# A two-layer graph attention kernel: who loads the adjacency matrix, and onto how many partitions at a time

## The chip, the cores and the metric

The kernel runs on one core of a Trainium2 chip. Its time is the device time of one execution in microseconds (us). The kernel before took 2251.49 us as the median of three runs (2243.89 to 2266.31); the execution that was profiled took 2266.05 us, of which the trace's span holds 2264.2 us.

## The reference, cut to what matters

Two attention layers over 8192 nodes with 128 features, the same adjacency matrix in both:

```python
h = jnp.maximum(_layernorm(x, axis=-1), 0.0)
x = x + _L0_gnn_ref(h, adj, ...)
h = jnp.maximum(_layernorm(x, axis=-1), 0.0)
x = x + _L1_gnn_ref(h, adj, ...)

def _L0_gnn_ref(node_features, adjacency_matrix, W, b_W, a_vec, b_a):
    h = node_features @ W.T + b_W
    a1, a2 = (a_vec[:D_OUT], a_vec[D_OUT:])
    e = (h @ a1)[:, None] + (h @ a2)[None, :] + b_a[0]
    e = jnp.where(e > 0, e, 0.2 * e)
    scores = jnp.where(adjacency_matrix > 0, e, jnp.float32(NEG_INF))
    attention = jax.nn.softmax(scores, axis=1)
    return attention @ h
```

`x` is 8192 x 128 float32, `adj` is 8192 x 8192 int32, 256 MB. The second layer differs in names only.

## The kernel before, in words

Since a score is the larger of two sums, each of a row's and a column's term, the exponential of a score is one of two products. So a layer needs no exponential per edge: each edge is a byte of a 0/1 mask in one of two stationary operands (`masks`: sum positive, sum negative), and TensorE multiplies the masks with rows of nodes that were scaled before (`node_rows`). One tile is 128 rows of the adjacency matrix against all 8192 columns: 64 chunks, two matmuls each.

The program has three parts. **Node phase**: for each of 64 tiles of 128 nodes, VectorE, GpSimd (a power, L423), TensorE and ScalarE normalise and project, and the rows go to device memory; each quarter of them comes back rearranged (`load_quadrant`, four loads of 516 KB). **Layer 0**: 64 tiles of adjacency. **Layer 1**: 64 tiles with masks that layer 0 has packed.

A tile of layer 0 works on four row groups r of 32 rows. Partition 32a + i holds row 32r + i of the tile and the columns of quarter a (2048 int32, 8 KB). ScalarE turns each group into bytes (`cast`, L600: `sign_a` from `adj_sb`). `adj_sb` has one buffer for each r and no second one, so a group can be loaded for the next tile once it has been cast for this one. VectorE joins `sign_a` with the sign of the score (`mask_bits`, L824), packs two tiles' masks into `pair_a` (`pack`, L833 on even tiles and L836 on odd ones), transposes blocks (`turn_bits`, L845) and splits the two masks (L853, L860), after which TensorE may start the tile (L538). ScalarE stores `pair_a`, 1 MB, once for two tiles (`store_pair`, L607), and the pack of the next even tile waits until that store has landed. `pair_a` has one buffer.

TensorE's result of a tile is finished on ScalarE (`part_one`, L619) and VectorE (L869 and on), and layer 0 also runs the node work of layer 1 for the finished tiles: VectorE's statistics and `ext` (L790), GpSimd's power (`node_step`, L423), its sum and copy and one scaled half of the rows (`node_rest`, L435, L436, L445), ScalarE's exponential and other half (`node_high`, L586, L588). In `layer_0_tile` ScalarE's order is: `part_one` of the tile before, the store on odd tiles, cast 0 of the tile two ahead, a copy, `z_sign`, cast 1, `z_sign`, cast 2, `node_high` of the tile two behind, cast 3. GpSimd's L445 needs the first result of that `node_high`.

Every engine runs its own list in the order written, with loops over two tiles (four in the node phase); only semaphores hold them. On SP, layer 0 is: for each r, wait for the cast of r and issue the four loads of that group for the next tile; then store and load `x`, and store the node rows. The adjacency of tile 0 is loaded in the node phase, one row group behind the row stores of tiles 16, 32, 35 and 48.

Of the kernel before, what the change touches and what calls it, by code (L numbers as in the profile page):

```python
# [27 lines left out]
TILE = 128  # L28
TILES = NODES // TILE
QUADS = 4  # L30
QROWS = 32
SPAN = NODES // QUADS
RGROUPS = TILE // QROWS
BYTES = 4
BLOCKS = SPAN // (QROWS * BYTES)
# [25 lines left out]
HEAD = 4  # L61
TAIL = 62
NODE_STEP = 4
QUAD_ORDER = (0, 2, 1, 3)


class Tile:
# [21 lines left out]
            eng.wait_ge(sem, self.t - back + 1)  # L89


def sweep(eng, body, trail=0, step=2, head=HEAD):

    end = TILES - step
    for k in range(head):
        body(Tile(k))
    with eng.Fori(head // step, end // step) as u:
        for k in range(step):
            body(Tile(k, u, step))
    for k in range(end, TILES + trail):  # L100
        body(Tile(k))


def gat_kernel(nc, x, adj, w_0, b_w_0, a_vec_0, b_a_0, w_1, b_w_1, a_1, out):
    F32, F16, I8, I32, U32, FP8 = (mybir.dt.float32, mybir.dt.float16, mybir.dt.int8, mybir.dt.int32,
                                   mybir.dt.uint32, mybir.dt.float8e4)
    ALU, ACT, AX = mybir.AluOpType, mybir.ActivationFunctionType, mybir.AxisListType
    ds = bass.ds
# [6 lines left out]
    with ExitStack() as ctx:  # L115
        def sb(name, shape, dt):
            return ctx.enter_context(nc.sbuf_tensor(name, shape, dt))
# [4 lines left out]
        def sem(name):  # L122
            return ctx.enter_context(nc.semaphore(name))


        adj_sb = sb("adj_sb", [128, RGROUPS, SPAN], I32)
        sign_a = sb("sign_a", [128, 2, NODES], I8)
        sign_z = sb("sign_z", [128, 2, NODES], I8)
        pair_a = sb("pair_a", [128, NODES], I8)
# [67 lines left out]
        setup_pe, setup_dve = sem("setup_pe"), sem("setup_dve")  # L197
        x_head, x_rest, rows_free = sem("x_head"), sem("x_rest"), sem("rows_free")
        adj_loaded = [sem(f"adj_loaded_{r}") for r in range(RGROUPS)]
        cast_done = sem("cast_done")  # L200
        packed, pair_stored, pair_loaded = sem("packed"), sem("pair_stored"), sem("pair_loaded")

        class LayerSems:
# [41 lines left out]

        @block.sync
        def _(sp):
            def load_adj(T, r):
                for a in QUAD_ORDER:
                    sp.nop(nofuse=True)  # L250
                    sp.dma_start(adj_sb[QROWS * a:QROWS * (a + 1), r, :],  # L251
                                 adj[ds(T.t * TILE + QROWS * r, QROWS), SPAN * a:SPAN * (a + 1)]) \
                      .then_inc(adj_loaded[r], 16)

            def load_x_old(l, T):
                if T.u is not None or T.k >= 2:
                    sp.wait_ge(S[l].fin, FIN * (T.t - 1))
                sp.nop(nofuse=True)
                sp.dma_start(x_old[:, T.p, :], x_src[l][ds(T.t * TILE, TILE), :]).then_inc(S[l].x_old[T.p], 16)
# [6 lines left out]
            def store_rows(l, T):  # L266
                sp.wait_ge(S[l].low, T.t + 1)
                sp.nop(nofuse=True)
                slot, _ = row_slot(l, T)
                sp.dma_start(rows_dram[l][ds(T.t, 1), :, :].rearrange("o p r -> p (o r)"), row_parts[:, slot, :]) \  # L270
                  .then_inc(S[l].rows_stored[slot], 16)
# [20 lines left out]
            def load_x_group(g):  # L292
                sp.dma_start(x_all[:, first * g:first * (g + 1), :], x_tiles[:, first * g:first * (g + 1), :]).then_inc(x_rest, 16)
# [6 lines left out]
                for g in range(VGROUPS):  # L300
                    load_rows(0, a, g)

            adj_after = [BLOCKS, 2 * BLOCKS, 2 * BLOCKS + 3, 3 * BLOCKS]
            for a in range(QUADS):
                for k in range(BLOCKS * a, BLOCKS * a + NODE_STEP):
                    store_rows(0, Tile(k))
                    if k in (0, 2):
                        load_x_group(2 + k // 2)
                    if k in adj_after:
                        load_adj(Tile(0), adj_after.index(k))  # L310
                if a:
                    load_quadrant(a - 1)
                with sp.Fori(BLOCKS // NODE_STEP * a + 1, BLOCKS // NODE_STEP * (a + 1)) as u:
                    for k in range(NODE_STEP):
                        store_rows(0, Tile(k, u, NODE_STEP))
# [10 lines left out]
                sp.dma_start(pair_a[:], mask_dram[ds(T.n, 1), :, :].rearrange("o p c -> p (o c)")).then_inc(pair_loaded, 16)  # L326

            def layer_0_tile(T):
                if T.plus(1).exists:
                    for r in range(RGROUPS):  # L330
                        sp.wait_ge(cast_done, RGROUPS * T.t + r + 1)
                        load_adj(T.plus(1), r)
                if T.plus(-3).exists:
                    store_x_new(0, T.plus(-3))
                    load_x_old(0, T.plus(-1))
                if T.plus(-4).exists:
                    store_rows(1, T.plus(-4))
# [58 lines left out]
        def _(pool):  # L396
# [5 lines left out]
                               pattern=[[-1, 128]], channel_multiplier=1).then_inc(ident_ready, 1)  # L402
# [3 lines left out]
            def build_picks():  # L406
                for r in range(RGROUPS):
                    pool.tensor_copy(pick_s[:, r, :].rearrange("p (a i) -> p a i", a=QUADS),
                                     ident[:, QROWS * r:QROWS * (r + 1)].unsqueeze(1).to_broadcast([128, QUADS, QROWS])) \
                        .then_inc(picks_ready, 1)  # L410
                for b in range(BLOCKS):
                    pool.tensor_copy(pick_t[:, b, :].rearrange("p (a i) -> p a i", a=QUADS),
                                     t_columns[:, b, :].unsqueeze(2).to_broadcast([128, QUADS, QROWS])).then_inc(picks_ready, 1)

            build_picks()
            nat_v = nat[:].rearrange("p (c t) -> p c t", c=2)

            def node_step(l, T):
# [28 lines left out]

            for l in range(LAYERS):
                if l:
                    pool.wait_ge(S[0].nat_ps, 1)  # L450
                    pool.wait_ge(S[0].coefs, 2)
                    pool.wait_ge(limits, n_limits)

                def body(T):
                    if l and T.u is None and T.k == TILES - 2:
                        pool.wait_ge(S[0].turned, TILES)
                        build_picks()
                    if T.exists:
                        node_step(l, T)
                    rest = T.plus(l - 1)  # L460
                    if rest.exists:
                        node_rest(l, rest)

                sweep(pool, body, trail=1 - l, step=[NODE_STEP, 2][l])


        @block.tensor
# [103 lines left out]
        def _(act):  # L571
# [22 lines left out]
            def cast(T, r):  # L594

                if r == 0 and (T.u is not None or T.k >= 2):
                    act.wait_ge(S[0].edge_bits, T.t - 1)
                    act.wait_ge(packed, T.t - 1)
                act.wait_ge(adj_loaded[r], 16 * QUADS * (T.t + 1))
                nc.scalar.activation(sign_a[:, T.p, SPAN * r:SPAN * (r + 1)], adj_sb[:, r, :], ACT.Sign, scale=-1.0) \  # L600
                  .then_inc(cast_done, 1)

# [647 lines left out]
```

## Time and profile before

| | us |
|---|---|
| median of three runs | 2251.49 |
| the profiled execution | 2266.05 |
| its span | 2264.2 |
| TensorE matmuls busy | 2015.0 (89%) |
| VectorE busy | 1664.7 (74%) |
| ScalarE busy | 1134.8 (50%) |
| GpSimd busy | 347.0 (15%) |
| node phase, about | 0 to 157 |
| layer 0, about | 157 to 1300 |
| layer 1, about | 1360 to 2264 |

A busy share is an average over three parts with different limits, so each part is read by itself: the DMA row of the page is full in layer 0 and nearly empty in layer 1. In the rows of groups, the number before a "mean ns of one" is the busy sum, and what stands behind the bar is the idle time of the engine just before such an instruction with what ended it. A wait that hangs on several semaphores is put down to the one that came last by the profile.

### The profile page before, as it was taken

How to read it: one execution, taken by the hardware profiler on the slowest of the kernel's cores; microseconds unless marked ns; L12 is line 12 of the kernel's file. 1: busy time of each engine (PE TensorE's matmuls, PEld its weight loads, DVE VectorE, ACT ScalarE, POOL GpSimd, SP SyncE). 2: the span in 40 equal slices, each digit the busy share in tenths (PEclk: the TensorE clock that was granted, in tenths of full speed). 3: DMA queues.
4: the chain of work that ended last, by engine and by line, in shares of the span. 5: the costliest groups of instructions: out<-in, count | busy, mean ns of one | idle time of the engine just before them, and what ended most of it. 6: DMA issues, size and time to landing. Idle time of an engine off the chain costs nothing.

```text
span 2264.2 us, 49373 instructions
## 1 busy us (share of the span) xinstructions
PE 2015.0 (89%) x16866; PEld 1710.1 (76%) x16866; DVE 1664.7 (74%) x2685; ACT 1134.8 (50%) x1097; POOL 347.0 (15%) x496
## 2 busy tenths in 40 slices
PE   5455889889998898988988979999999999999998
PEld 3234677777777777777877868888888888888887
DVE  6564778778878777787787767777777777777774
ACT  4455667777767676676777433322222223333331
POOL 6440122212222222222222210000000000000000
PEclk9997899999999999999999989999999999999999
DMA  5659999999999999999999681111111111111110
GB/s 145 161 141 243 254 292 280 288 294 309 309 304 269 282 277 278 286 273 288 282 285 296 180 189 47 46 46 46 46 46 46 46 46 46 46 46 46 45 45 11
DMA packets 121683, 390.99 MB, mean 173 GB/s; under 512 B 25137, under 2 KB 74545, under 8 KB 80689
## 3 DMA queue, kind: packets, MB, share of 16 engines
q1 hardware_dynamic: 117040, 357.01, 58.2%
q10 hardware_dynamic: 4608, 33.56, 3.7%
q8 instruction: 18, 0.29, 0.1%
q14 instruction: 17, 0.13, 0.0%
HBM read 331.62 MB, written 58.85 MB: 172 GB/s over the span
## 4 chain that ended last, share of the span: by engine, by line
PE 59%; DMA 25%; DVE 5%; issue 4%; ACT 3%; SPq 2%; DVEq 0%; ACTq 0%; POOL 0%; POOLq 0%
PE acc L538 58%; DMA adj_sb<-in_adj_dram 12%; DMA mask_bytes<-pair_a 11%; DVE masks L845 2%; DMA node_rows<-row_parts 2%; ACT sign_a L600 2%; SPq L251 1%; DVE ext L790 1%; ACT part_a L619 1%; PE ps_h L490 0%; ACT b_and_d L586 0%; ACT row_parts L588 0%; DMA masks<-in_x_dram 0%; DVE row_parts L797 0%; SPq L277 0%
## 5 line engine op out<-in xcount | busy, mean ns | idle before, releaser
L538 PE MATMUL acc<-node_rows,masks 128*128 128x258 f16 x16384 | 1907.9, 278 | 133.7 <-ACT part_a L619 76.0
L538 PEld LDWEIGHTS acc<-node_rows,masks 128*128 128x128 fp8e4 x16384 | 1624.3, 99 | 396.6 <-issue 142.1
L600 ACT ACTIVATE sign_a<-adj_sb 128x2048 int8<-128x2048 int32 x256 | 487.4, 1904 | 142.3 <-DMA adj_sb<-in_adj_dram 137.7
L613 ACT ACTIVATE sign_z<-t_row,neg_s 128x2048 int8<-128x2048 f32 x256 | 503.9, 1994 | 1.0 <-DVE masks L845 1.0
L619 ACT ACTIVATE part_a<-acc,coef_a 128x258 f32<-128x258 f32 x128 | 60.1, 470 | 721.4 <-PE acc L538 721.4
L809 DVE TENSOR_SCALAR sign_z<-t_row,neg_s 128x2048 int8<-128x2048 f32 x256 | 327.0, 1279 | 7.4 <-issue 6.8
L845 DVE STREAM_TRANSPOSE masks<-sign_z 128x2048 uint32<-128x2048 uint32 x128 | 295.0, 2305 | 0.1
L869 DVE SCALAR_TENSOR_TENSOR part_ac<-acc,coef_c,part_a 128x258 f32<-128x258 f32 x128 | 62.1, 485 | 297.8 <-ACT part_a L619 297.6
L435 POOL TENSOR_TENSOR h_sum<-h_sum,ext 128x128 f32<-128x128 f32 x126 | 113.1, 898 | 795.5 <-DVE ext L790 791.8
L833 DVE TENSOR_SCALAR pair_a<-sign_a 128x2048 uint32<-128x2048 uint32 x32 | 39.3, 1227 | 179.8 <-DMA mask_bytes<-pair_a 179.8
L824 DVE SCALAR_TENSOR_TENSOR sign_z<-sign_z,sign_a 128x2048 uint32<-128x2048 uint32 x64 | 146.3, 2285 | 19.7 <-ACT sign_z L613 19.7
L853 DVE TENSOR_SCALAR masks<-masks 128x2048 uint32<-128x2048 uint32 x128 | 155.9, 1218 | 0.1
L860 DVE TENSOR_SCALAR masks<-masks 128x2048 uint32<-128x2048 uint32 x128 | 155.8, 1217 | 0.1
L824 DVE SCALAR_TENSOR_TENSOR sign_z<-sign_z,pair_a 128x2048 uint32<-128x2048 uint32 x64 | 146.3, 2286 | 1.4 <-ACT sign_z L613 1.3
L423 POOL TENSOR_TENSOR rstd<-var_eps,minus_half 128x1 f32<-128x1 f32 x128 | 125.3, 980 | 139.8 <-DVE var_eps L726 139.5
L490 PE MATMUL ps_h<-w_ext,centred_t 128*128 128x133 f32 x256 | 78.0, 397 | 73.1 <-ACT centred_t L575 69.5
L490 PEld LDWEIGHTS ps_h<-w_ext,centred_t 128*128 128x128 f32 x256 | 51.9, 253 | 94.0 <-ACT centred_t L575 71.8
L797 DVE SCALAR_TENSOR_TENSOR row_parts<-ext,b_and_d,row_parts 128x129 f16<-128x129 f32 x256 | 89.0, 349 | 44.6 <-ACT row_parts L588 44.2
L586 ACT ACTIVATE b_and_d<-ext 128x2 f32<-128x2 f32 x128 | 25.6, 200 | 179.3 <-DVE ext L790 132.0
L445 POOL TENSOR_SCALAR row_parts<-ext,b_and_d 128x129 f16<-128x129 f32 x64 | 75.3, 1176 | 17.3 <-ACT b_and_d L586 17.2
L836 DVE SCALAR_TENSOR_TENSOR pair_a<-sign_a,pair_a 128x2048 uint32<-128x2048 uint32 x32 | 73.0, 2282 | 0.0
L485 PE MATMUL ps_t<-ident,centred 128*128 128x128 f32 x128 | 49.4, 388 | 19.6 <-DVE centred L723 18.4
(81 smaller groups left out, 580.2 us busy)
## 6 DMA issues: line engine op xcount, KB each, us to landing
adj_sb<-in_adj_dram SPq DMA_DIRECT2D x1024, 256.0 KB, 10.4
mask_bytes<-pair_a ACTq DMA_DIRECT2D x32, 1024.0 KB, 10.8
pair_a<-mask_bytes SPq DMA_DIRECT2D x32, 1024.0 KB, 4.8
node_rows<-row_parts SPq DMA_DIRECT2D x128, 129.0 KB, 8.1
node_rows<-node_rows SPq DMA_DIRECT2D x32, 516.0 KB, 12.3
x_old<-in_x_dram SPq DMA_DIRECT2D x64, 64.0 KB, 11.9
x_after_layer<-x_new SPq DMA_DIRECT2D x64, 64.0 KB, 12.3
x_old<-x_after_layer SPq DMA_DIRECT2D x64, 64.0 KB, 1.8
```

What stands on the lines that cost most here:

```text
L423: pool.tensor_tensor(rstd[:, T.p, :], var_eps[:, T.p, :], minus_half[:], ALU.pow).then_inc(S[l].rstd, 1)
L435: pool.tensor_tensor(h_sum[:], h_sum[:], ext[:, T.p, 0:DIM], ALU.add).then_inc(S[l].h_sum, 1)
L490: pe.matmul(ps_h[:, 0:EXT], centred_t[:, T.p, :], w_ext[l][:], start=True, stop=True).then_inc(S[l].h_raw, 1)
L538: mm = pe.matmul(acc[T.p][s][:, 0:ROW], stationary[s][:, c // BYTES, c % BYTES, :], node_rows[:, c, ROW * s:ROW * (s + 1)], start=(c == 0) ...
L600: nc.scalar.activation(sign_a[:, T.p, SPAN * r:SPAN * (r + 1)], adj_sb[:, r, :], ACT.Sign, scale=-1.0) \
L613: nc.scalar.activation(sign_z[:, T.p, SPAN * r:SPAN * (r + 1)], t_row[:], ACT.Sign, scale=-1.0, bias=neg_s[:, ds(RGROUPS * T.t + r, 1)]).t ...
L797: ins = nc.vector.scalar_tensor_tensor(out=row_parts[:, slot, ROW * s + PART:ROW * (s + 1)], in0=ext[:, T.p, 0:PART], scalar=b_and_d[:, T. ...
L809: nc.vector.tensor_scalar(sign_z[:, T.p, SPAN * r:SPAN * (r + 1)], t_row[:], neg_s[:, ds(RGROUPS * T.t + r, 1)], -1.0, ALU.is_gt, ALU.mult) \
L824: nc.vector.scalar_tensor_tensor(out=bits, in0=bits, scalar=LOW_Z_WORD[T.p], in1=edges, op0=ALU.bitwise_xor, op1=ALU.bitwise_and).then_inc ...
L845: nc.vector.transpose(g2[:, T.p, :].bitcast(U32).rearrange("p (b r i) -> p r b i", r=RGROUPS, i=QROWS), sign_z[:, T.p, :].bitcast(U32).rea ...
L853: nc.vector.tensor_scalar(g1[:, T.p, :].bitcast(U32), words, SHIFT_G1[T.p], EDGE_WORD, ALU.logical_shift_left, ALU.bitwise_and).then_inc(S ...
L860: nc.vector.tensor_scalar(words, words, SHIFT_G2[T.p], EDGE_WORD, ALU.logical_shift_left, ALU.bitwise_and).then_inc(S[l].g_ready, 1)
```

## The change

The adjacency loads move from SP's queue to GpSimd's. One indirect DMA loads a whole row group, 1 MB onto 128 partitions: the matrix is seen as 32768 rows of 2048 elements, and partition p takes the row whose number stands in `adj_index` for it. The numbers are made once (an `iota` and three small corrections) in two copies, and after a tile's loads the other copy is moved on by two tiles. The bytes, their places and the single buffer per row group are as before; 1024 loads become 256.

```diff
-            def load_adj(T, r):
-                for a in QUAD_ORDER:
-                    sp.nop(nofuse=True)
-                    sp.dma_start(adj_sb[QROWS * a:QROWS * (a + 1), r, :],
-                                 adj[ds(T.t * TILE + QROWS * r, QROWS), SPAN * a:SPAN * (a + 1)]) \
-                      .then_inc(adj_loaded[r], 16)
...
-                    if k in adj_after:
-                        load_adj(Tile(0), adj_after.index(k))
...
             def layer_0_tile(T):
-                if T.plus(1).exists:
-                    for r in range(RGROUPS):
-                        sp.wait_ge(cast_done, RGROUPS * T.t + r + 1)
-                        load_adj(T.plus(1), r)
                 if T.plus(-3).exists:
...
+            def load_adj(T):
+
+                pool.wait_ge(index_ready, QUADS + T.t)
+                for r in range(RGROUPS):
+                    if T.u is not None or T.k:
+                        pool.wait_ge(cast_done, RGROUPS * (T.t - 1) + r + 1)
+                    pool.nop(nofuse=True)
+                    pool.indirect_dma_start(out=adj_sb[:, r, :], out_offset=None, in_=adj_rows_of_2048,
+                                            in_offset=bass.IndirectOffsetOnAxis(ap=adj_index[:, T.p, r:r + 1], axis=0)) \
+                        .then_inc(adj_loaded[r], 16)
+                if T.u is None and T.k == 0:
+                    pool.engine_nop().then_inc(index_ready, 1)
+                else:
+                    pool.tensor_scalar(adj_index[:, 1 - T.p, :], adj_index[:, 1 - T.p, :], float(2 * QUADS * TILE), 1.0,
+                                       ALU.add, ALU.mult).then_inc(index_ready, 1)
...
             for l in range(LAYERS):
                 if l:
+                    load_adj(Tile(1))
                     pool.wait_ge(S[0].nat_ps, 1)
                     pool.wait_ge(S[0].coefs, 2)
                     pool.wait_ge(limits, n_limits)
+                    for k in range(2, LOADS_AHEAD):
+                        load_adj(Tile(k))
 
                 def body(T):
...
+                    if l == 0 and T.u is None and T.k == HEAD - 1:
+                        load_adj(Tile(0))
+                    if l and T.plus(LOADS_AHEAD).exists:
+                        load_adj(T.plus(LOADS_AHEAD))
                     if T.exists:
                         node_step(l, T)
```

`LOADS_AHEAD` is 4. The lines of the file move by 19 behind the GpSimd part (ScalarE's cast is L600 before and L619 after).

GpSimd's loop of layer 0 before, one of its two tiles (a row is a line of the kernel, the operation, result and operands, and the semaphores it waits for; the names ending in 1 are layer 1's node work):

```order
L423 TENSOR_TENSOR rstd<-var_eps,minus_half 128x1 [waits var_eps_1,ext_1]
L435 TENSOR_TENSOR h_sum<-h_sum,ext 128x128 [waits ext_1,h_sum_1]
L436 ISA
L436 COPY nat<-ext 128x2
L445 TENSOR_SCALAR row_parts<-ext,b_and_d 128x129 [waits b_and_d_1,rows_stored_1_1]
```

The same loop now, from the end of the even tile (L457 is L445 of before) to where the odd tile's power (L435, before L423) follows:

```order
L457 TENSOR_SCALAR row_parts<-ext,b_and_d 128x129 [waits rows_stored_1_0]
L414 REGISTER_ALU
L417 ISA [waits index_ready]
L419 DMA adj_sb<-in_adj_dram,adj_index 128x2048 [waits cast_done]
L417 REGISTER_ALU
L419 DMA adj_sb<-in_adj_dram,adj_index 128x2048 [waits cast_done]
L417 REGISTER_ALU
L419 DMA adj_sb<-in_adj_dram,adj_index 128x2048 [waits cast_done]
L417 REGISTER_ALU
L419 DMA adj_sb<-in_adj_dram,adj_index 128x2048 [waits cast_done]
L425 TENSOR_SCALAR adj_index<-adj_index 128x4
L432 REGISTER_ALU
```

The four loads stand between one tile's L457, ahead of which GpSimd waits for ScalarE's `b_and_d`, and the next tile's L435.

SP's loop of layer 0 before, the last row group of one tile and what follows it:

```order
L251 ISA [waits cast_done]
L251 DMA adj_sb<-in_adj_dram 32x2048
L251 ISA
L251 DMA adj_sb<-in_adj_dram 32x2048
L251 ISA
L251 DMA adj_sb<-in_adj_dram 32x2048
L251 ISA
L251 DMA adj_sb<-in_adj_dram 32x2048
L262 ISA
L264 ISA [waits fin_0]
L264 DMA x_after_layer<-x_new 128x128
L259 ISA [waits fin_0]
```

And one tile of it now:

```order
L258 ISA [waits fin_0]
L258 DMA x_after_layer<-x_new 128x128
L253 ISA [waits fin_0]
L253 DMA x_old<-in_x_dram 128x128
L264 ISA [waits low_1]
L264 DMA node_rows<-row_parts 128x516
```

SP waits for no cast any more.

## Rows read from the trace of the kernel before

**Rows 1.** The page: busy time, slices of the span, DMA.
```profile
PE 2015.0 (89%) x16866; PEld 1710.1 (76%) x16866; DVE 1664.7 (74%) x2685; ACT 1134.8 (50%) x1097; POOL 347.0 (15%) x496
...
DMA  5659999999999999999999681111111111111110
```

**Rows 2.** Stretches: us, busy by engine (instructions), clock, DMA share, GB/s.
```profile
197.00:490.00 293.00, 244.69 (x2049) 205.86 (x2050) 223.72 (x327) 204.28 (x160) 53.80 (x57) 0.94 1.02 277
490.00:1290.00 800.00, 718.30 (x6032) 610.38 (x6030) 629.80 (x970) 561.13 (x459) 193.14 (x185) 0.94 1.00 282
...
1364.00:2264.00 900.00, 890.73 (x7962) 777.36 (x7960) 651.92 (x806) 256.91 (x183) 0.00 (x0) 1.00 0.13 44
```

**Rows 3.** Chain of waits in two stretches: start us, us, what.
```profile
377.22 12.93 DMA adj_sb<-in_adj_dram
390.17 1.92 ACT sign_a L600
...
663.82 10.86 DMA mask_bytes<-pair_a
...
698.25 11.29 DMA mask_bytes<-pair_a
```

**Rows 4.** Cast 3 of tiles 1, 3 and 63, from the timeline.
```profile
191.34 1.91 ACT L600 ACTIVATE sign_a<-adj_sb 128x2048 int8<-128x2048 int32 x1 [2.67 <-DMA adj_sb<-in_adj_dram]
...
230.13 1.91 ACT L600 ACTIVATE sign_a<-adj_sb 128x2048 int8<-128x2048 int32 x1 [2.54 <-DMA adj_sb<-in_adj_dram]
...
1275.92 1.89 ACT L600 ACTIVATE sign_a<-adj_sb 128x2048 int8<-128x2048 int32 x1
```

**Rows 5.** Timeline around one even tile: start us, us, engine, line.
```profile
698.77 1.91 ACT L600 ACTIVATE sign_a<-adj_sb 128x2048 int8<-128x2048 int32 x1 [0.24 <-issue]
...
706.33 1.90 ACT L600 ACTIVATE sign_a<-adj_sb 128x2048 int8<-128x2048 int32 x1
...
709.57 1.23 DVE L833 TENSOR_SCALAR pair_a<-sign_a 128x2048 uint32<-128x2048 uint32 x1 [6.75 <-DMA mask_bytes<-pair_a]
...
715.12 1.21 DVE L860 TENSOR_SCALAR masks<-masks 128x2048 uint32<-128x2048 uint32 x1
...
716.58 4.03 PE L538 MATMUL acc<-node_rows,masks 128*128 128x258 f16 x18 [4.00 <-ACT part_a L619]
```

**Rows 6.** The same timeline, the tile after it, ScalarE and GpSimd.
```profile
717.60 1.33 POOL L423 TENSOR_TENSOR rstd<-var_eps,minus_half 128x1 f32<-128x1 f32 x1 [1.03 <-DVE var_eps L726]
...
728.11 1.34 POOL L435 TENSOR_TENSOR h_sum<-h_sum,ext 128x128 f32<-128x128 f32 x1 [9.18 <-DVE ext L790]
728.49 0.19 ACT L586 ACTIVATE b_and_d<-ext 128x2 f32<-128x2 f32 x1
729.63 1.35 POOL L445 TENSOR_SCALAR row_parts<-ext,b_and_d 128x129 f16<-128x129 f32 x1
```

**Rows 7.** The page: DMA issues, KB each, median us from issue to landing.
```profile
adj_sb<-in_adj_dram SPq DMA_DIRECT2D x1024, 256.0 KB, 10.4
mask_bytes<-pair_a ACTq DMA_DIRECT2D x32, 1024.0 KB, 10.8
pair_a<-mask_bytes SPq DMA_DIRECT2D x32, 1024.0 KB, 4.8
...
x_old<-x_after_layer SPq DMA_DIRECT2D x64, 64.0 KB, 1.8
```

**Rows 8.** GpSimd in the node phase, and what VectorE waits for there.
```profile
18.04 0.55 POOL L435 TENSOR_TENSOR h_sum<-h_sum,ext 128x128 f32<-128x128 f32 x1 [0.51 <-DVE ext L790]
...
30.86 0.29 DVE L710 BATCH_NORM_STATS2 stats<-masks 128x6 f32<-128x128 f32 x1 [5.92 <-DMA masks<-in_x_dram]
```

**Rows 9.** Chain of waits in the node phase.
```profile
91.75 15.59 DMA node_rows<-row_parts
```

**Rows 10.** Timeline where layer 0 opens, GpSimd and SP.
```profile
154.97 0.25 POOL L436 COPY nat<-ext 128x2 f32<-128x2 f32 x1
...
162.72 37.55 SPq L251 DMA_DIRECT2D adj_sb<-in_adj_dram  x35
```

More of the change, by code:

```diff
@@ L63 @@
 NODE_STEP = 4
-QUAD_ORDER = (0, 2, 1, 3)
+LOADS_AHEAD = 4
 class Tile:
@@ L89, in wait_before, with sweep @@
             eng.wait_ge(sem, self.t - back + 1)
-def sweep(eng, body, trail=0, step=2, head=HEAD):
-    end = TILES - step
+def sweep(eng, body, trail=0, step=2, head=HEAD, tail=None):
+    end = TILES - (tail or step)
     for k in range(head):
@@ L126, in gat_kernel @@
         adj_sb = sb("adj_sb", [128, RGROUPS, SPAN], I32)
+        adj_index = sb("adj_index", [128, 2, RGROUPS], I32)
         sign_a = sb("sign_a", [128, 2, NODES], I8)
@@ L199, in gat_kernel @@
         adj_loaded = [sem(f"adj_loaded_{r}") for r in range(RGROUPS)]
-        cast_done = sem("cast_done")
+        cast_done, index_ready = sem("cast_done"), sem("index_ready")
         packed, pair_stored, pair_loaded = sem("packed"), sem("pair_stored"), sem("pair_loaded")
@@ L301, in load_quadrant @@
                     load_rows(0, a, g)
-            adj_after = [BLOCKS, 2 * BLOCKS, 2 * BLOCKS + 3, 3 * BLOCKS]
             for a in range(QUADS):
@@ L415, in _ @@
             build_picks()
+            pool.iota(adj_index[:].rearrange("p b r -> p (b r)"), pattern=[[QUADS * TILE, 2], [QUADS * QROWS, RGROUPS]], base=0,
+                      channel_multiplier=QUADS).then_inc(index_ready, 1)
+            pool.wait_ge(index_ready, 1)
+            for a in range(1, QUADS):
+                part = adj_index[QROWS * a:QROWS * (a + 1), :, :].rearrange("p b r -> p (b r)")
+                pool.tensor_scalar(part, part, float(a - QUADS * QROWS * a), 1.0, ALU.add, ALU.mult).then_inc(index_ready, 1)
+                pool.wait_ge(index_ready, a + 1)
+            adj_rows_of_2048 = adj.rearrange("n (a c) -> (n a) c", a=QUADS)
+            def load_adj(T):
[12 more added lines that the diff above has]
+                                       ALU.add, ALU.mult).then_inc(index_ready, 1)
             nat_v = nat[:].rearrange("p (c t) -> p c t", c=2)
@@ L462, in body @@
                         node_rest(l, rest)
-                sweep(pool, body, trail=1 - l, step=[NODE_STEP, 2][l])
+                sweep(pool, body, trail=1 - l, step=[NODE_STEP, 2][l], tail=[NODE_STEP, LOADS_AHEAD][l])
         @block.tensor
@@ L598, in cast @@
                     act.wait_ge(packed, T.t - 1)
-                act.wait_ge(adj_loaded[r], 16 * QUADS * (T.t + 1))
+                act.wait_ge(adj_loaded[r], 16 * (T.t + 1))
                 nc.scalar.activation(sign_a[:, T.p, SPAN * r:SPAN * (r + 1)], adj_sb[:, r, :], ACT.Sign, scale=-1.0) \
```

## The prediction

> **What bounds the kernel now.** Start with the page [rows 1]: a TensorE busy for 89% says little here, while the DMA row reads 9 (90% or more) from the fourth slice to the twenty-second, which is layer 0, and 1 behind it. Then the stretches [rows 2]. Layer 1 is TensorE's: 64 tiles in 900 us, 14.06 us each, at full clock and a DMA share of 0.13. It has no adjacency load and the change cannot touch it. Layer 0 has a DMA share of 1.00 to 1.02 at 277 to 282 GB/s, and a clock of 0.94.
>
> The chain of waits [rows 3] splits layer 0 in two. Up to about 490 us it runs in a ring: cast 3 of a tile (1.92), SP's issue, a load that takes about 13 us to land (12.93 in the row), cast 3 of the next tile. From there to 1290 us a 1 MB mask store of 10.9 to 11.3 us comes once in two tiles, 34.4 us apart (663.82 to 698.25): VectorE's pack of the even tile stands 6.75 us until the store has landed, its last mask ends at 716.33, and TensorE starts at 716.58 after 4.00 us of idleness [rows 5]. That row names ScalarE's `part_a`, but the code wants only the `part_a` of two tiles before, so I take the mask, which ended 0.25 us earlier, as what let TensorE go. From cast 3 of tile 3 to cast 3 of tile 63 it is (1275.92 - 230.13) / 60 = 17.43 us a tile [rows 4]. Both halves are transfers that share the DMA engines: the loads crowd the store and the store crowds the loads.
>
> A tile moves 4 MB of adjacency, half a mask store (0.5 MB), `x` in and out (64 KB each) and 129 KB of rows: 4.75 MB in 17.2 us (half of 34.4), or 3.6 us per MB. For comparison, layer 1's `pair_a` load has the shape of the new loads, 1 MB as 8 KB on each of 128 partitions, and with nothing beside it lands in 4.8 us; 64 KB land in 1.8 [rows 7]. So 960 KB more cost 3.0 us, 3.2 us per MB.
>
> **Part 1: when the load is issued.** This is where I expect the change to be decided. Before, SP issues the load of group 0 as soon as cast 0 has freed the buffer, and there remains almost a tile's time for it. Now it is issued by GpSimd, in program order behind L445 (L457 in the new file), which scales a node's rows and waits for ScalarE's `b_and_d`. ScalarE computes `b_and_d` only behind cast 2. Loads of groups 0, 1 and 2 whose buffers have long been free stand behind it. That closes a ring, once per tile:
>
> - GpSimd issues group 0's load, and it lands: 4.8 us if it is alone, by the `pair_a` load [rows 7], plus what software issue costs over SP's, which no row shows. From below nothing; from above, two GpSimd instructions of layer 0, 2.7. I take one, 1.3, since the issue walks 128 partitions as L435 (1.34) and L445 (1.35) do [rows 6].
> - ScalarE from the start of cast 0 to the end of cast 2, with a copy and two `z_sign` between: 698.77 to 708.23, 9.46 us [rows 5]. Nothing can be taken out, since it runs without a gap.
> - `b_and_d` 0.19 and L445 1.35 [rows 6], about 1.6 with the semaphores.
>
> Sum: 4.8 + 1.3 + 9.5 + 1.6 = 17.2 us. ScalarE does cast 3 and `part_one` while the load is under way, and both are hidden. On odd tiles ScalarE issues the mask store behind cast 3 and `part_one`, about 3 us after cast 2 ends, and GpSimd has issued group 0 after 1.6 + 1.3 us: the two start together. If the store's MB goes entirely beside group 0, it adds 3.2 us; if behind it, nothing. The store lands in 10.8 us beside loads against the 4.8 of a lone MB [rows 7], so sharing is real; I take 2.4, three quarters. The mean is 17.2 + 1.2 = **18.4 us a tile**, 0.97 more than now, and for the 60 tiles from 3 to 63 that is +58 us. Between the ends: 11.1 + 4.8 = 15.9 us (neither issue nor store costs anything) and 11.1 + 4.8 + 2.7 + 1.6 = 20.2 us (two instructions' worth of issue, the store's whole 3.2 on every other tile).
>
> The other limits stay under this. TensorE is busy 718.3 of 800 us, 15.7 us a tile at 17.43, part of it at the lower clock. The DMA engines' load is 4.75 MB by 3.2 to 3.6, 15.2 to 17.1 us. VectorE is busy 629.8 of 800 us, 13.7 us a tile [rows 2].
>
> **Part 2: what 128 partitions bring.** Before, four loads of 256 KB land in 10.4 us each in a queue, so no row tells the rate that the matrix could have. The bracket is 3.6 us per MB as now and 3.2 as the `pair_a` load has it. It shortens the ring of the first stretch, which this change replaces by the ring of part 1 anyway. Over the stretches bound by these loads and stores the trace moves 277 and 282 GB/s [rows 2].
>
> The Trainium skill ("SBUF — State Buffer", "Door 1: The DMA port swizzle") says that a transfer onto 32 partitions reaches 8 of 16 ports, with 189 GB/s measured at 1 MB, and that only a single transfer over all 128 reaches every port. This trace does not agree for quarters in a row: with them it moves half as much again. By that rule the matrix would have been at half rate and the change would win, which is the first rival; by the rows a spread MB gains 0.4 us at most.
>
> **Part 3: GpSimd and VectorE.** L435 takes 0.55 us in the node phase [rows 8] and 1.34 in layer 0 [rows 6], beside VectorE's long instructions. So GpSimd is slowed there, and its four issues would be too; that is why the price above is 1.3 and not 0.6. Its own list is four issues at 1.3, the index at 1.3, L423 1.33, L435 1.34, L436 0.25 and L445 1.35 [rows 6, 10], 10.8 us a tile, under 17. The power L423, now behind the issues, is due when VectorE reaches `ext`; between the end of L423 and the next `ext` the rows leave 728.11 - 718.93 = 9.2 us [rows 6], more than the 6.5 of issues and index.
>
> The Trainium skill ("SBUF — State Buffer", the warning that VectorE blocks DMAs) says that a VectorE instruction in a two-port mode keeps GpSimd from writing its DMAs' descriptors, and that DMAs from SP or ScalarE are immune. L435's two durations agree that GpSimd is held up there; for a DMA no row here shows it. It speaks against this change, and what it would do is the second rival.
>
> **Part 4: the beginning.** Node phase: three times the chain runs through a row store that lands late, the longest 15.59 us [rows 9], because 1 MB of adjacency (2 in that one) and 2 MB of rows stand ahead in SP's queue. Without the adjacency that is 4 x 3.6 = 14 us less. Against that, all 4 MB now come at about 21 us, just before VectorE waits for `x` until 30.86 [rows 8]: between nothing and the same 14 us, and the four issues hold up GpSimd's power by 5 us, inside that wait. I take the 14, together 0. Opening of layer 0: SP's loads of tile 1 begin at 162.72, GpSimd could issue from 155.2 [rows 10], beside 2 MB of rows: 6 MB at 3.6 land by 177, cast 3 of tile 1 was at 191.34 [rows 4], -13. Tiles 2 and 3 come without the ring (GpSimd issues them with no node work between): 4.5 MB by 3.6, 16.3 against (230.13 - 191.34) / 2 = 19.4, -6. Sum of the part: about **-20**, with ends -34 (`x` is not delayed) and +5 (the opening gains nothing and the issues are not covered).
>
> SP loses 1024 issues, which are credited with nothing, since the transfer behind each hides them. Its `x` loads and stores now share the engines with another queue instead of standing in line. The removed pack wait (6.75 us) does not come back as time, since the ring is longer than what it held up.
>
> **Sum.** -20 + 58 = +38 us: 2266.05 becomes 2304 for such an execution, and from the median, which is 14.6 lower, **2290 us**, 1.7% slower.
>
> **Rivals.**
> 1. *Faster.* The ring is shorter than now: software issue costs about as much as SP's, and the store falls behind group 0's load. Then a tile is 15.9 to 17.2 us, middle 16.6, and 60 tiles save 50, with the beginning 70 us: 2181. For it: the store bound more than half of layer 0, and that is gone; the first stretch was bound by loads, and if their shape held them back, spread loads leave the engines free for the store. Against it: 9.5 us of ScalarE work and 4.8 us of landing stand in one ring and leave only 1.5 us to lose. It decides from issue plus store under 1.5 us a tile. By the port rule of the Trainium skill (its page on SBUF) it would come out this way. Chance 0.28.
> 2. *Much slower.* Each issue on GpSimd takes 2.5 us or more under VectorE, or the indirect loads move at less than 1 MB in 3.6. A tile is then 20 to 21 us: -20 + 60 x 3 = +160, 2410. For it: the stretching of L435. Against it: right behind L445 VectorE waits for ScalarE's `part_a`, so the first issue at least finds it idle. By the Trainium skill's warning on blocked descriptors (same page) it would come out this way. Chance 0.17.
> 3. *Nothing.* The ring comes out at 17.4 to 17.9 us, and the beginning pays for it: 2231 to 2260. This also covers that loads spread over 128 partitions are as fast as the four quarters in a row, so that one full DMA queue is exchanged for another. Chance 0.10.
>
> **How the numbers follow.** About 1% (22 us) is what this measurement can tell from no change. The forecast has 0.45, of which 0.08 lies within 1%. Faster 0.28, same 0.10 + 0.08 = 0.18, slower 0.37 + 0.17 = 0.54. The forecast's own range is 2255 to 2325 (ring 17.8 to 19.0). To leave out no more than 2 in 10, the range reaches down to 2190, which takes in most of the first rival, and up to 2410, the second.
>
> **What would show it.** Right: ScalarE's cast 0 waits for `adj_sb` on nearly every tile, 3 us or more, and casts 1 and 2 hardly; GpSimd's first load of a tile starts right behind L457; cast 3 to cast 3 is 17.5 to 19 us; VectorE's L833 no longer waits for the store; the DMA row in layer 0 falls below 9. Wrong: the wait at cast 0 stays under 2 us (rival 1); GpSimd's issues last over 2 us or all four casts wait (rival 2); cast 3 of tile 1 is not near 178 us, or `x` is late by more than 14 us (part 4).

## The result, and the profile after

The changed kernel took 2299.14 us as the median of four runs (2297.34 to 2300.41), beside 2255.56 us for the kernel before in four runs: a ratio of 1.022, with a 95% interval of 1.017 to 1.026. The forecast was 2290 us, slower by 1.7%.

The page of the changed kernel, its busy row, slices and the three queues that moved data:

```profile
PE 2033.5 (88%) x16866; PEld 1719.1 (75%) x16866; DVE 1674.4 (73%) x2685; ACT 1124.7 (49%) x1097; POOL 763.3 (33%) x819
...
DMA  5558777777677777767777581111111111111110
...
q0 software_dynamic: 36864, 268.45, 29.7%
q1 hardware_dynamic: 67888, 88.51, 13.1%
q10 hardware_dynamic: 4608, 33.56, 4.6%
```

Against [rows 1], the DMA row of layer 0 has fallen from 9 to 7 while the kernel became slower: the transfers got cheaper, and the DMA engines stand idle part of the time. GpSimd's busy time has doubled. The stretches say the same (answers to [rows 2], same columns):

```profile
197.00:490.00 293.00, 256.15 (x2118) 215.80 (x2117) 224.66 (x338) 195.66 (x159) 168.02 (x141) 0.94 0.72 271
490.00:1290.00 800.00, 693.21 (x5694) 582.94 (x5693) 603.09 (x912) 532.38 (x436) 464.88 (x393) 0.93 0.71 272
```

The DMA share went from 1.00 to 0.71 in the long stretch for nearly the same rate (282 and 272 GB/s), and TensorE's matmuls there from 6032 to 5694: fewer tiles in the same 800 us. Where the time goes is in the waits (engine and line, who it waited for, us in total, times, longest):

```profile
ACT sign_a L619 <- DMA adj_sb<-in_adj_dram,adj_index: 320.3, 67, 8.4
...
POOL row_parts L457 <- ACT b_and_d L605: 199.5, 59, 5.1
...
DVE pair_a L852 <- DMA mask_bytes<-pair_a: 36.0, 30, 5.1
```

ScalarE's casts now wait 4.8 us each, 67 times, which is about once in a tile (before it was 137.7 us in 98 waits). GpSimd waits for ScalarE's `b_and_d`, 59 times. VectorE's pack (L833 before, L852 now) waits 36.0 us where it waited 179.8. A ring of two engines and a transfer has taken the place of the store: GpSimd issues the load, ScalarE casts it and then computes `b_and_d`, and GpSimd waits for that before the next load. One pair of tiles in the timeline (start us, us, engine, line; in brackets the idle time before and its end):

```profile
702.51 0.38 POOL L457 TENSOR_SCALAR row_parts<-ext,b_and_d 128x129 f16<-128x129 f32 x1 [2.86 <-ACT b_and_d L605]
...
703.39 1.60 POOL L419 DMA_INDIRECT adj_sb<-in_adj_dram,adj_index  x1 [0.50 <-issue]
...
704.44 0.34 ACTq L626 DMA_DIRECT2D mask_bytes<-pair_a  x1
...
711.89 1.91 ACT L619 ACTIVATE sign_a<-adj_sb 128x2048 int8<-128x2048 int32 x1 [7.03 <-DMA adj_sb<-in_adj_dram,adj_index]
...
719.45 1.90 ACT L619 ACTIVATE sign_a<-adj_sb 128x2048 int8<-128x2048 int32 x1
721.25 0.19 ACT L605 ACTIVATE b_and_d<-ext 128x2 f32<-128x2 f32 x1
...
721.64 0.38 POOL L457 TENSOR_SCALAR row_parts<-ext,b_and_d 128x129 f16<-128x129 f32 x1 [5.09 <-ACT b_and_d L605]
...
722.76 1.68 POOL L419 DMA_INDIRECT adj_sb<-in_adj_dram,adj_index  x1 [0.74 <-issue]
...
729.28 1.91 ACT L619 ACTIVATE sign_a<-adj_sb 128x2048 int8<-128x2048 int32 x1 [3.74 <-DMA adj_sb<-in_adj_dram,adj_index]
...
739.97 1.59 POOL L419 DMA_INDIRECT adj_sb<-in_adj_dram,adj_index  x1 [0.50 <-issue]
```

From the first load's issue to the next tile's: 722.76 to 739.97 is 17.21 us without a store (an even tile's group 0), 703.39 to 722.76 is 19.37 us with the store issued a microsecond behind (an odd one's). Over tiles 6 to 62 of the trace the two kinds take 17.18 and 19.59 us in the mean. Over the layer (answers to [rows 4]: cast 3 of tile 3 and of tile 63):

```profile
208.42 1.91 ACT L619 ACTIVATE sign_a<-adj_sb 128x2048 int8<-128x2048 int32 x1 [0.53 <-DMA adj_sb<-in_adj_dram,adj_index]
...
1310.56 1.90 ACT L619 ACTIVATE sign_a<-adj_sb 128x2048 int8<-128x2048 int32 x1
```

Tile 3 is reached 230.13 - 208.42 = 21.7 us sooner than before. From there 60 tiles take 18.37 us each instead of 17.43, +56.3 us, and what follows is equal (2264.2 - 1275.9 = 988.3 us before, 2298.6 - 1310.6 = 988.0 now). -21.7 + 56.3 = +34.6, against a difference of the two spans of 34.4 us.

### The profile page after: what moved, and what is told of

Its sections match the earlier page's. It is cut to its first block, busy times and chain, and to the rows that moved or that the text cites. A ratio compares the mean times of both kernels' runs of the same rounds, so it can differ in the third digit from the quotient of the medians.

```text
span 2298.6 us, 46859 instructions
## 1 busy us (share of the span) xinstructions
PE 2033.5 (88%) x16866; PEld 1719.1 (75%) x16866; DVE 1674.4 (73%) x2685; ACT 1124.7 (49%) x1097; POOL 763.3 (33%) x819
## 4 chain that ended last, share of the span: by engine, by line
PE 48%; DMA 21%; issue 14%; ACT 11%; DVE 3%; SPq 1%; POOL 1%; DVEq 0%; POOLq 0%; ACTq 0%
PE acc L557 47%; DMA adj_sb<-in_adj_dram,adj_index 16%; ACT sign_a L619 6%; ACT sign_z L632 3%; DMA node_rows<-row_parts 3%; PE ps_h L509 1%; DMA masks<-in_x_dram 1%; DVE ext L809 1%; ACT centred_t L594 1%; SPq L271 0%; DMA mask_bytes<-pair_a 0%; ACT b_and_d L605 0%; DVE masks L864 0%; ACT row_parts L607 0%; ACT part_a L638 0%
## 5 line engine op out<-in xcount | busy, mean ns | idle before, releaser
L619 ACT ACTIVATE sign_a<-adj_sb 128x2048 int8<-128x2048 int32 x256 | 486.3, 1901 | 320.4 <-DMA adj_sb<-in_adj_dram,adj_index 320.3
L419 POOL DMA_INDIRECT adj_sb<-in_adj_dram,adj_index x256 | 424.9, 1660 | 124.1 <-issue 94.6
L828 DVE TENSOR_SCALAR sign_z<-t_row,neg_s 128x2048 int8<-128x2048 f32 x256 | 327.5, 1281 | 5.9 <-issue 5.3
L864 DVE STREAM_TRANSPOSE masks<-sign_z 128x2048 uint32<-128x2048 uint32 x128 | 294.9, 2304 | 0.1
L509 PE MATMUL ps_h<-w_ext,centred_t 128*128 128x133 f32 x256 | 88.2, 441 | 193.8 <-ACT centred_t L594 186.3
L843 DVE SCALAR_TENSOR_TENSOR sign_z<-sign_z,sign_a 128x2048 uint32<-128x2048 uint32 x64 | 146.3, 2285 | 4.2 <-ACT sign_z L632 4.2
L843 DVE SCALAR_TENSOR_TENSOR sign_z<-sign_z,pair_a 128x2048 uint32<-128x2048 uint32 x64 | 146.3, 2286 | 1.4 <-ACT sign_z L632 1.3
L435 POOL TENSOR_TENSOR rstd<-var_eps,minus_half 128x1 f32<-128x1 f32 x128 | 105.6, 827 | 9.9 <-DVE var_eps L745 4.5
L457 POOL TENSOR_SCALAR row_parts<-ext,b_and_d 128x129 f16<-128x129 f32 x64 | 26.5, 414 | 199.5 <-ACT b_and_d L605 199.5
L809 DVE SCALAR_TENSOR_TENSOR ext<-ps_h,rstd,bias 128x133 f32<-128x133 f32 x128 | 43.4, 339 | 44.7 <-PE ps_h L509 44.5
```

The lines of the kernel that those rows point to most:

```text
L419: pool.indirect_dma_start(out=adj_sb[:, r, :], out_offset=None, in_=adj_rows_of_2048, in_offset=bass.IndirectOffsetOnAxis(ap=adj_index[:, ...
L435: pool.tensor_tensor(rstd[:, T.p, :], var_eps[:, T.p, :], minus_half[:], ALU.pow).then_inc(S[l].rstd, 1)
L509: pe.matmul(ps_h[:, 0:EXT], centred_t[:, T.p, :], w_ext[l][:], start=True, stop=True).then_inc(S[l].h_raw, 1)
L828: nc.vector.tensor_scalar(sign_z[:, T.p, SPAN * r:SPAN * (r + 1)], t_row[:], neg_s[:, ds(RGROUPS * T.t + r, 1)], -1.0, ALU.is_gt, ALU.mult) \
L843: nc.vector.scalar_tensor_tensor(out=bits, in0=bits, scalar=LOW_Z_WORD[T.p], in1=edges, op0=ALU.bitwise_xor, op1=ALU.bitwise_and).then_inc ...
L864: nc.vector.transpose(g2[:, T.p, :].bitcast(U32).rearrange("p (b r i) -> p r b i", r=RGROUPS, i=QROWS), sign_z[:, T.p, :].bitcast(U32).rea ...
```

## The experiments

Twelve kernels were built, each run four times (six for the two with three early groups, ten for the changed kernel with the small store). "Tile" is (cast 3 of tile 63 - cast 3 of tile 3) / 60 in each one's trace; a ratio is to the kernel before on the same chip.

| kernel | us | ratio, 95% interval | tile, us |
|---|---|---|---|
| changed kernel | 2299.1 | 1.022, 1.017 to 1.026 | 18.37 |
| three groups early | 2104.2 | 0.934, 0.931 to 0.938 | 15.09 |
| group 0 early | 2114.3 | 0.939, 0.935 to 0.944 | 15.33 |
| three early, tile 0 later | 2103.9 | 0.932, 0.929 to 0.936 | 15.10 |
| 0.95 us ahead of the loads | 2314.1 | 1.026, 1.020 to 1.031 | 18.57 |
| 0.95 us behind the loads | 2300.5 | 1.019, 1.013 to 1.024 | 18.38 |
| 2.8 us ahead of the loads | 2427.1 | 1.081, 1.077 to 1.086 | 20.46 |
| changed, small store | 2237.0 | 0.994, 0.992 to 0.997 | 17.42 |
| before, small store | 2203.1 | 0.976, 0.969 to 0.983 | 15.87 |
| SP, 1 MB on 128 partitions | 2134.1 | 0.947, 0.943 to 0.952 | 15.66 |
| the same, strided source | 2134.1 | 0.950, 0.947 to 0.954 | 15.60 |
| SP, quarters, contiguous | 2275.5 | 1.013, 1.006 to 1.020 | 17.52 |
| SP, 256 KB on 128 partitions | 2111.6 | 0.941, 0.937 to 0.945 | 15.24 |

**Is it the place of the loads in GpSimd's list?** Two kernels move loads ahead of the waits, each for the tile five ahead instead of four; behind L457 that is the same tile as before. The first, shortened (the call in the loop's body goes):

```diff
-LOADS_AHEAD = 4
+LOADS_AHEAD = 5
 def node_rest(l, T):
+    load_adj(T.plus(LOADS_AHEAD), [0, 1])
     pool.wait_ge(S[l].ext, T.t + 1)
 ...
+    load_adj(T.plus(LOADS_AHEAD), [2])
     pool.wait_ge(S[l].b_and_d, T.t + 1)
 ...
     pool.tensor_scalar(row_parts[...], ...).then_inc(S[l].high_d, 1)
+    load_adj(T.plus(LOADS_AHEAD), [3])
```

> The changed kernel with GpSimd's loads taken out of one block: groups 0 and 1 of the next tile are issued ahead of the wait for ext, group 2 ahead of the wait for ScalarE's b_and_d, group 3 behind the scaled rows (L457). Ring theory (a tile is GpSimd's issue behind L457, landing, ScalarE's casts 0 to 2, b_and_d, L457: 18.37 us): the ring is gone, a tile falls to what engines and transfers allow, 15.5 to 16.5 us, and the run takes 2299 - 60 x 2.2 = 2165 us (2150 to 2190). Rival 1, software-issued loads move too slowly or take too long to issue: no more than 1% changes, 2280 to 2300. Rival 2, eight more microseconds of GpSimd work beside VectorE slow the tile, wherever they stand: no change.

It took 2104 us, 8.5% less than the changed kernel and 6.6% less than the kernel before. Direction and place are as the ring says; the size is well past the 2150 to 2190 us expected. The stretch and the timeline of this kernel:

```profile
490.00:1100.00 610.00, 595.33 (x5296) 516.85 (x5294) 556.40 (x849) 497.61 (x404) 427.87 (x362) 1.00 0.88 330
```

```profile
699.13 1.56 POOL L416 DMA_INDIRECT adj_sb<-in_adj_dram,adj_index  x1
...
701.98 1.03 POOL L416 DMA_INDIRECT adj_sb<-in_adj_dram,adj_index  x1 [1.29 <-ACT sign_a L630]
703.00 1.90 ACT L630 ACTIVATE sign_a<-adj_sb 128x2048 int8<-128x2048 int32 x1
...
709.10 1.80 POOL L416 DMA_INDIRECT adj_sb<-in_adj_dram,adj_index  x1 [0.15 <-issue]
```

Loads now leave GpSimd soon after casts have freed the buffers (the second row waited for a cast), and no cast of the steady tiles waits a microsecond or more. TensorE is busy 98% of the stretch at full clock, and a tile of 15.09 us is near the 14.06 us of layer 1 plus the node matmuls. The kernel has become TensorE's in both layers, and moves 330 GB/s at a DMA share of 0.88.

The second moves group 0 alone (`[0]` ahead of `ext`, `[1, 2, 3]` behind L457):

> Only group 0's load is issued early (ahead of the wait for ext); groups 1 to 3 stay behind L457 as in the changed kernel. Ring theory: the ring now runs through group 1, 6.5 us of issue and landing + 5.6 us from cast 1 to the end of cast 2 + 1.3 = 13.4 us, shorter than TensorE's tile, so most of the gain of the run with three early groups is there already: 2160 to 2200 us. If the ring holds for every group (the order of the loads does not matter, their number behind L457 does), about a quarter of that gain: 2265. Rivals of slow transfers or of GpSimd's load: 2280 to 2300.

2114 us, below the expected range too: 185 of the 195 us come with one load of four. It is group 0's load behind L457 that closed the ring, as the arithmetic of 13.4 us for group 1 said. What waits now is cast 1, more than 1 us in 56 of 60 tiles, and cast 0 in 7. The three loads still there cost about 10 us, and GpSimd's added work is all still present.

**A dose on the ring and beside it.** A memset in a buffer of its own, in one kernel ahead of the four loads, in its twin behind them:

```diff
 if l and T.plus(LOADS_AHEAD).exists:
+    pool.memset(spare[:], 0.0)       # one kernel
     load_adj(T.plus(LOADS_AHEAD))
+    pool.memset(spare[:], 0.0)       # the other
```

> The changed kernel with one more GpSimd instruction, a memset of 128 x 1024 float32 in a buffer of its own, between L457 and the first load of each steady tile. Ring theory: its duration d (1 us or a little more; the trace will tell) lengthens every tile: 2299 + 60 d, about 2365 us. Rival, transfers bound the tile and GpSimd has slack: 2299. Rival, GpSimd's work beside VectorE costs wherever it stands: the same loss as in the twin with the memset elsewhere.

> The twin: the same memset behind the four loads and the index update, ahead of the power L435. Ring theory: off the ring, 2299 us within 0.5%. Rival, GpSimd's work beside VectorE costs wherever it stands: as slow as the kernel with the memset ahead of the loads.

Beside the ring it costs nothing (2300.5). On the ring it cost 15 us where 57 were expected (0.95 us by its trace, 60 times). The trace of the kernel with the dose shows where the rest went:

```profile
727.41 0.38 POOL L458 TENSOR_SCALAR row_parts<-ext,b_and_d 128x129 f16<-128x129 f32 x1 [4.78 <-ACT b_and_d L607]
...
727.74 0.94 POOL L477 MEMSET spare<- 128x1024 f32 x1
...
728.86 1.38 POOL L420 DMA_INDIRECT adj_sb<-in_adj_dram,adj_index  x1 [0.18 <-issue]
```

From the end of the scaled rows to the load there are 1.07 us with the memset and were 0.50 to 0.74 without, so half of it filled an issue gap. From the load's issue to cast 0 the tiles then take 0.2 to 0.3 us less in the mean. On even tiles the first issue is shorter (1.41 us for 1.67 in the mean, here 1.38 for 1.68), on odd ones it is longer (1.91 for 1.60) and the load lands sooner all the same, so this second part is seen and not explained. In all 0.75 of 0.95 us were absorbed. A longer dose, a copy of 128 x 3072 to int8 at the same place, should then cost its length less a constant:

> The memset between L457 and the first load gave 0.2 us a tile for 0.95 us of work, since the first load's issue got shorter beside it and an issue gap of 0.5 to 0.7 us was filled. Here a longer GpSimd instruction (a copy of 128 x 3072 int8, about 3 us) stands there. Ring theory with 0.7 us absorbed once: 2299 + 60 x (d - 0.7), 2430 us for d = 3. If GpSimd had slack at that place and the small dose showed it: under 2330.

2427.1 us. Its trace has these casts 3 of tile 3 and tile 63:

```profile
210.00 1.91 ACT L621 ACTIVATE sign_a<-adj_sb 128x2048 int8<-128x2048 int32 x1 [0.50 <-DMA adj_sb<-in_adj_dram,adj_index]
...
1437.82 1.90 ACT L621 ACTIVATE sign_a<-adj_sb 128x2048 int8<-128x2048 int32 x1
```

The copy takes 2.74 us in the median and 2.79 in the mean, and the tile grew by 20.46 - 18.37 = 2.09 us, its mean length less 0.7. With d = 2.74 to 2.79 the expected formula gives 2421 to 2424. From the small dose to the long one, 1.84 us more of work made the tile 1.90 longer: the slope is the ring's, and both doses lost the same 0.7 to 0.75 us. The growth is not even, though: even tiles grew by 3.1 us (17.18 to 20.30) and odd ones by 1.1 (19.59 to 20.70). The later loads meet the store at another moment, which may be why; it was not tried.

**What does the store cost?** The store and its load in layer 1 cut from 8 KB to 64 bytes a partition:

```diff
-act.dma_start(mask_dram[ds(T.n, 1), :, :]..., pair_a[:])
+act.dma_start(mask_dram[ds(T.n, 1), :, 0:64]..., pair_a[:, 0:64])
```

> The changed kernel with the mask store (and the load of it in layer 1) cut from 1 MB to 8 KB in all, 64 bytes a partition; it leaves out most of the packed mask. Ring theory: odd tiles lose the 2.2 us by which the store lengthens group 0's landing (8.5 against 6.5 us), every tile takes the even tile's 17.2 us: 2299 - 60 x 1.1 = 2233 us. If the store runs in time that is idle anyway: 2299.

2237.0 us for 2233 expected, and a tile of 17.42 us, close to the even tile's 17.21. The mean over odd tiles fell from 19.59 to 17.77 us, over even ones it stayed at 17.18. The other side, the same cut in the kernel before:

> The kernel before with the mask store and its load cut to 64 bytes a partition; it leaves out most of the packed mask. If the store bounded the second part of layer 0, the wait of 6.75 us in two tiles goes and the loads have the engines to themselves: tiles of 15.6 us instead of 17.4, 2251 - 60 x 1.8 = 2145 us. If the loads bound everything anyway: a tenth fewer bytes, 2225.

This one is not settled in size. Its four runs spread from 2167 to 2239 us, and the profiled one is the fastest of them, with a tile of 15.87 us. All four lie below the lowest of the eleven runs of the kernel before beside them (2244), so the cut does something, but the median lies between the two expectations. In its trace the queue is still full (share 1.03) and ScalarE waits 161 us for loads, so the loads were the next bound. Nor did the pack's wait go as expected: VectorE still waits 99 us in 31 times (179.8 before), since the 8 KB store lands in 8.8 us in the median beside those loads, against 10.8 for 1 MB. What held the pack up was mostly the full queue, and not the store's own bytes.

**What was fast: the partitions, the source or the size?** The kernel with three early groups came out 61 us under its expectation (2104 for 2165). Its 330 GB/s are 3.2 us per MB, the low end of the prediction's 3.2 to 3.6, and that at a DMA share of 0.88, so the transfers must be cheaper still. Four kernels keep SP as the issuer, with its order and waits, and vary the load alone. The first:

```diff
-for a in QUAD_ORDER:
-    sp.dma_start(adj_sb[QROWS * a:QROWS * (a + 1), r, :],
-                 adj[ds(T.t * TILE + QROWS * r, QROWS), SPAN * a:SPAN * (a + 1)])
+sp.dma_start(adj_sb[:, r, :],
+             adj.rearrange("n (a c) -> (n a) c", a=QUADS)[ds(T.t * (QUADS * TILE) + 128 * r, 128), :])
```

> The kernel before with SP issuing each row group as one direct load of the same contiguous MB onto 128 partitions (partition p takes the p-th 8 KB), so issuer, order and times of issue are as before and only the shape is that of the change. It leaves out the arrangement of the rows, so the masks belong to other edges. If the shape frees the transfers (3.2 instead of 3.6 us per MB or better): the ring of loads in the first stretch and the wait for the store shrink, 2170 to 2210 us. If quarters in a row were as fast as a spread MB: 2240 to 2265, no change against before.

2134 us, below the 2170 to 2210 expected: the shape alone is worth 5% when issuer, order and waits stay. The next takes `adj[ds(T.t * TILE, TILE), SPAN * r:SPAN * (r + 1)]` as the source:

> As the run with one direct 1 MB load from SP per row group, but the MB is 128 rows of 8 KB that stand 32 KB apart in device memory, the run before had them in one piece. It leaves out the arrangement of the rows. If the spread over 128 partitions made that run fast: the same, 2134 us (2120 to 2150). If it was the contiguous source: back towards the kernel before, 2220 to 2260.

And four quarters again, each from one contiguous piece (`[... + 128 * r + QROWS * a, QROWS]`):

> The other half of that question: SP loads four quarters of 256 KB onto 32 partitions each, as the kernel before, but each quarter is one contiguous piece of the same contiguous MB. It leaves out the arrangement of the rows. If partitions decide: as the kernel before, 2235 to 2265 us. If the source decides: 2134.

The strided source changes nothing (2134.1) and the quarters bring the old time back, even 1.3% more (2275.5, and 10 us above the range; why was not tried). It is the spread over 128 partitions and not the source. The last keeps the partitions and cuts the size, four loads of 512 columns:

> SP loads each row group in four DMAs of 256 KB, each over all 128 partitions with 2 KB a partition. It leaves out the arrangement of the rows. If the number of partitions decides and not the size of a DMA: near 2134 us, 2130 to 2170 for four times the issues and smaller pieces. If the size of a DMA (1 MB against 256 KB) decides: as the kernel before, 2235 to 2265.

2111.6 us, faster than with 1 MB and below the expected range: the size of a DMA is not what made 1 MB fast. The same stretch, 490 to 1100 us, of the kernels before, with 1 MB, with contiguous quarters and with spread 256 KB:

```profile
490.00:1100.00 610.00, 547.99 (x4617) 466.13 (x4615) 476.17 (x736) 433.24 (x352) 146.33 (x140) 0.94 1.02 288
```

```profile
490.00:1100.00 610.00, 578.97 (x5083) 500.94 (x5081) 529.61 (x817) 478.11 (x388) 163.85 (x156) 0.99 0.87 317
```

```profile
490.00:1100.00 610.00, 537.50 (x4619) 456.26 (x4618) 479.48 (x736) 437.75 (x352) 130.32 (x140) 0.98 1.03 289
```

```profile
490.00:1100.00 610.00, 593.78 (x5283) 516.10 (x5281) 548.80 (x848) 496.33 (x404) 170.27 (x161) 1.00 0.98 329
```

Quarters fill the DMA engines (1.02, 1.03) at 288 and 289 GB/s, wherever they read from. Spread 1 MB loads move 317 GB/s at 0.87 and are then not the bound: TensorE is busy 95% of the stretch. The strided kernel's stretch has 318 GB/s at 0.89.

The Trainium skill ("SBUF — State Buffer", "Door 1: The DMA port swizzle") gives the rule that only a transfer over all 128 partitions reaches all ports. These runs agree in direction, and disagree with half the rate for 32 partitions: with quarters the core moved 288 GB/s. The Trainium skill ("DMA: Bandwidth & Descriptors", "Rules for kernel authors") also asks for 1 MiB or more a DMA beside 128 partitions, for maximum bandwidth. Here the kernel with 256 KB was faster than the one with 1 MB, 2111.6 against 2134.1, but its DMA engines worked more for each byte (329 GB/s at 0.98, against 317 at 0.87), so these runs do not refute the rule as one on bandwidth.

**Tile 0's loads.** They moved from node tile 3 to node tile 15 in the kernel with three early groups:

> The kernel with three early groups, and tile 0's four loads issued at node tile 15 instead of 3. In the changed kernel VectorE waited for x until 41.0 us instead of 30.9, since 4 MB of adjacency came just ahead of x. With the loads later: x lands by 31 us again, -10 us against the kernel with three early groups; a part comes back if row stores then stand beside the loads. Expected 6 to 10 us less than that kernel. Rival, other transfers pay the same 4 MB wherever they stand: no difference.

No difference (2103.9 against 2104.2), as the rival had it. The half that concerns `x` came true in the trace: VectorE waits for it until 32.05 us instead of 41.38. But GpSimd's last copy of the node phase ends at 154.0 instead of 156.8, so 6.5 of the 9.3 us are lost again before layer 0. The chain shows part of it in a row store of 7.13 us where there was one of 1.84.

## Why the prediction was right, step by step

**The ring (part 1)** was right as a mechanism and to 0.03 us in its sum: 18.4 forecast, 18.37 measured. Its terms were less exact, and their errors cancel, so that closeness is luck.

- Issue and landing of group 0, 4.8 + 1.3 = 6.1 us: 6.52 on the even tile (6.49 in the mean of even tiles). The issue itself took 1.68, and the landing from its end on 4.84, the `pair_a` load's duration.
- ScalarE's casts 0 to 2, 9.46: 9.47 (729.28 to 738.75).
- `b_and_d`, scaled rows and semaphores, 1.6: 1.22 behind the even tile's cast 2 and 1.41 behind the odd one's. L457 takes 0.38 us where L445 took 1.35 [rows 6]: it no longer stands behind the sum and copy, and no long VectorE instruction runs beside it.
- The store, 2.4 us on odd tiles: 19.37 - 17.21 = 2.2. The run with the small store took 0.95 us off the mean tile (1.2 was the term).

That group 0's load is the one that counts, and not GpSimd's work as such, is shown by group 0 moved alone and by the dose behind the loads.

**What 128 partitions bring (part 2)** was mis-sized: "a spread MB gains 0.4 us at most". Over 610 us before, 288 GB/s at a full queue is 3.6 us per MB. The three runs with spread loads from SP take 1.8 to 2.2 us off the tile of 4.75 MB, which is 0.4 to 0.5 per MB already, and TensorE is then busy 95 to 97%. With three early groups 3.2 us per MB come at a share of 0.88; an estimate for a full queue is their product, 2.8, and the changed kernel's 272 GB/s at 0.71 (3.9 us per MB) give 2.7. So the gain is nearer 0.8 than 0.4. The bracket's lower end came from one load that was alone and cannot show what a queue of them reaches. The error did no harm to the forecast, since the ring hid the gain. For the repaired kernel it did, in part: 2165 expected, 2104 measured. The bracket's lower end would have given 4.75 x 3.2 = 15.2 us a tile there, near the 15.09 measured, but the expectation took 16.2. The first rival named this gain, but gave it 2181 with the ring still in place; with the ring, even a store that costs nothing left 17.4 us a tile.

**GpSimd and VectorE (part 3).** Two rows of the changed kernel, the first in the node phase, the second beside VectorE's 2.28 us mask instruction (706.80 to 709.08):

```profile
22.78 0.93 POOL L419 DMA_INDIRECT adj_sb<-in_adj_dram,adj_index  x1 [0.30 <-issue]
```

```profile
707.10 2.79 POOL L419 DMA_INDIRECT adj_sb<-in_adj_dram,adj_index  x1 [0.30 <-issue]
```

The issue is 0.93 us undisturbed and 1.66 in the mean of 256, up to 3.7. What runs beside it decides. In the trace 45 issues start while a mask instruction (L843) runs, and 39 of them end 0.81 or 0.82 us behind its end, whether they started 0.3 or 1.0 us into it: GpSimd gets on only when VectorE is through. Beside nothing (30 issues) the mean is 0.94 us, beside L828 (121) 1.60. The second rival's mechanism exists, but its price is 0.7 us a tile on the ring, since only the first issue stands on it (1.63 in the mean). GpSimd's own list came to 464.88 of 800 us, 10.7 us a tile, for 10.8 forecast.

The Trainium skill's warning ("SBUF — State Buffer", that VectorE blocks DMAs of GpSimd) agrees with these two rows in that GpSimd's issue is lengthened. The row of 2.79 us stands beside an instruction with two inputs in SBUF, of which the warning does not speak. The Trainium skill ("SBUF — State Buffer", "Who interferes with whom") does name such instructions as rivals of GpSimd's reads.

**The beginning (part 4)**: -20 forecast, -21.7 measured. VectorE waited for `x` until 41.01 us instead of 30.86, 10 us and not 14, and the three late row stores (12.05, 12.13 and 12.04 us in the chain) gave back 7 and not 14 (they were 13.60, 15.59 and 14.01). 0 in sum was nearly right: GpSimd's last copy of the node phase ends 1.2 us later (156.4 for 155.2). Cast 3 of tile 1 came at 176.1 us (177 to 178 forecast).

**The last step**, from the profiled execution to the median, is where most of the 9 us between 2290 and 2299 arise. The profiled execution was forecast at 2304 and took 2300.41. But it was then taken as typical that an execution lies 14.6 us above its median, as the one before did. The kernel before spreads over 22 us, while the changed kernel's four runs lie within 3.1 us.

Of the marks set, two were not met as written. VectorE's pack still waits for the store, but 1.2 us a time instead of 5.8. Cast 0 waits in all 60 steady tiles, but for 3 us or more in 48 of them; the others, even tiles without a store, wait 1.8 us or more.

## What to carry to other kernels

When a load moves to another engine's queue, write down what stands ahead of it in that queue and what that waits for; if the chain comes back to the load, its length is a floor for the period, however free the DMA engines are. Buffers that were free early are worth nothing behind such a wait, and moving the one load that closes the ring can be the whole repair: here one of four, 185 us. The gain of a better transfer shows only after that; a falling DMA row beside a growing time says that it is there and unused.

## What the runs showed that was not expected

- At a full queue, with loads onto 32 partitions in turn the core moved 288 GB/s, contiguous source or not; with loads over 128 partitions it moved 317 to 330 GB/s at shares of 0.87 to 0.98.
- Loads of 256 KB over 128 partitions (2 KB pieces) beat loads of 1 MB (8 KB pieces), 2111.6 against 2134.1 us. The mask store beside them landed in 8.1 against 9.1 us in the median. Why was not tried.
- An indirect load of 128 rows of 8 KB costs GpSimd 0.93 us alone and 1.66 in the mean beside VectorE, with a gap of 0.3 us between two and 0.5 to 0.7 ahead of the first. Other GpSimd work put ahead of the first was free for 0.7 us, about half a microsecond of it in that gap.
- A VectorE instruction with two inputs in SBUF holds up an indirect load's issue until it has ended: 39 of 45 such issues ended 0.8 us behind it.
